# One semaphore step per slot from TensorE in place of one per product, exponent and gather sum, in a vision-tower kernel

## The chip, the cores and the metric

The kernel runs on one core of a Trainium2 chip. The time is the device time of one launch in microseconds, median of the runs shown. TensorE (PE) does the matmuls, ScalarE (ACT) the activations and most evictions, VectorE (DVE) the elementwise work and the searches, GpSimd (POOL) issues the indirect gathers, and SyncE (SP) issues the other DMAs. Each engine runs its own instruction stream; they meet at semaphores only.

## The reference, cut to what matters

There are 64 images of 256 tokens with 64 channels. Each goes through three blocks: a token attention over 4x4 windows (`_L0_tok_ref`), a bidirectional selective scan (`_L0_attn_ref`) and a product-key memory attention (`_L0_ffn_ref`):

```python
h = _L0_tok_ref(x, ...)
h = h + _L0_attn_ref(_layernorm(h), ...)
h = h + _L0_ffn_ref(_layernorm(h), ...)
# in _L0_ffn_ref, for each of 8 heads:
kv_scores, indices = _pk(x, Wq_pk, pk_keys)
k = jnp.einsum('bnhk,bnhkd->bnhd', kv_scores, keys_table[ind])
v = jnp.einsum('bnhk,bnhkd->bnhd', kv_scores, values_table[ind])
out = softmax(causal(q @ k.T)) @ v
```

The third block fills most of the kernel: for each head and token, 16 rows of a table of 4096 are weighted and summed.

## The kernel before

The work is cut into periods of 56 slots, one period per image. In a period every engine works on three images at once: the third block of image b (lead 0), the end of the second block and the search of the third for image b+1, and the first two blocks of image b+2. The tables `FIRST`, `SECOND` and `OWN` say in which slot each engine does which piece of those.

Three and a half of the eight heads are *dense*: instead of gathering rows, TensorE multiplies a table of weights with all rows of the value table. One slot s of this is a chain over two engines:

- `overs` (L907, called o below), the count product: 96x512 bf16 into the bank `zd_ps[s % 2]`. It waits for the keys of the slot (`moving`, loaded by SP) and for the weights of slot s-2, which free the bank.
- `over_limit` (L1158, l below) on ScalarE, in the same bank.
- `exponents` (L913, z below), a second product into that bank, after l. It stands one slot later.
- `weights` (L1164, w below) on ScalarE, the exponential, after z.
- `product_part` (L890, and L896 in the half head at the end; d below), two fp32 products with the table rows `rowtab`, two slots later.

So TensorE's slot s is: z of s-1, o of s, d of s-2, then in 36 of the 56 slots the sums of one gathered part (`gather_sums`, L926, g below), then a stage of the attention over a finished head (`attention`, L940 to L967), then what the tables say. ScalarE's slot s is: w of s-1, in some slots the eviction `keep` (L1171) or `keep_gathered` of a finished head, l of s, a stage of the attention, and the rest.

TensorE tells the others of its progress with four semaphores of the dense and gathered part: `over_mm` steps at each o, `z_ready` at each z, `dense_done` at the second product of each d, and `summed` at the last product of each g. Who waits for them:

- l waits for `over_mm`; w for `z_ready` and for `dense_done` of two slots before (the `weight` buffer); `keep` for `dense_done`; `keep_gathered` for `summed`.
- SP's `load_keys` of slot s (L614 and L617) waits for `z_ready` of slot s-4, whose buffer of four it takes; it stands three slots ahead of its use. `load_tile` (L592) waits for `dense_done`.
- POOL's `gather_image` (L695): before the four gathers of a part it waits for `summed` of the part six before it (`RING` = 6).
- DVE's `spread_weights` waits for `summed` of the previous image.

SP's queue also carries, at slot 13, the load of an image three periods ahead (`load_image`, L578 to L580, three DMAs, 2 MB in all), and behind it in the same queue the keys of slot 16. The stage of slot 47 on TensorE, L814, waits for the end of DVE's scans (L1485).

Of the kernel before, what the change touches and what calls it, by code (L numbers as in the profile page):

```python
# [13 lines left out]
P = 128  # L14
# [21 lines left out]
DENSE = 3  # L36
# [20 lines left out]
WINDOW = (7, 3, 4, 0, 5, 1, 6, 2)  # L57
WSLOTS = 7
CARRIED = 2
# [19 lines left out]
FIRST = """  # L79
0 v.ps a.sq2  # L80
1 a.sq3
2 a.sq0
3 a.sq1
4 p.kv0 a.kv0
5 p.rf v.rf
6 p.kv1 a.kv1 p.kv2 a.kv2
7 p.kv3 a.kv3 p.kv4 a.kv4
8 p.kv5 a.kv5
9 p.kv6 a.kv6 p.kv7 a.kv7
10 p.kv8 a.kv8  # L90
11 p.kv9 a.kv9 p.kv10 a.kv10
12 p.kv11 a.kv11
13 v.var
14 a.rs0
15 v.nw0
16 p.t0 a.t0
17 p.q v.q0
18 v.q1
19 v.q2
20 a.sc  # L100
21 v.pv0
22 v.pv1
23 v.pv2
25 p.t1 a.t1
26 p.pj v.h1
27 a.rs1
28 v.nw1
29 p.t2 a.t2
30 p.xz a.ez
31 v.uz0  # L110
32 a.sg
33 v.uz1
34 p.xd a.xd p.dt a.dt0
35 a.dt1
36 v.dl
37 a.dc0
38 a.dc1 v.B0
39 a.dc2 v.sf0
40 a.dc3 v.sb0
41 a.dc4 v.B1 v.sf1  # L120
42 a.dc5 v.sb1
43 a.dc6 v.B2 v.sf2
44 a.dc7 v.sb2
45 v.B3 v.sf3
46 v.sb3
# [12 lines left out]
59 p.bk
60 v.h2
"""  # L140

SECOND = """
5 v.n0
6 v.n1 a.n
7 p.tb a.tb
8 p.s0 a.s0
9 v.T0 v.T1
10 v.T2 v.T3 p.s1 a.s1
11 v.T4 v.T5 p.s2 a.s2
12 v.T6  # L150
13 v.T7 v.T8 p.s3 a.s3
14 v.T9 v.T10
15 v.T11
16 v.T12 v.T13
19 v.T14
20 v.T15 v.T16
23 v.T17 v.T18
24 v.T19 v.cp v.i a.cp
25 v.pr0 v.L0 v.L1
26 v.L2 v.L3  # L160
27 v.wd v.pr1
28 a.wd
29 v.wx v.sel v.A0 v.G0
30 a.ln p.A0 a.hi0
31 v.A1 v.G1
32 v.re0 v.e0 a.mi0
33 v.G2 p.A1 a.hi1
34 v.e1 v.lo0
35 v.G3 v.re1 a.mi1
36 v.lo1 p.e0 a.e0  # L170
37 v.G4 v.e2 p.e1 a.e1
38 v.wg v.e3 p.e2 a.e2
39 a.wg p.e3 a.e3
40 v.wh
41 a.l2
44 v.R2
46 v.R3
47 v.X5 v.wb0
49 v.R4 v.R5
50 v.A2 v.A3  # L180
51 v.selh
52 v.R6 v.R7
53 v.wb1 v.e4 p.A2 a.hi2
54 v.R8 v.re2 a.mi2
55 v.e5 v.lo2 p.e4 a.e4
"""

OWN = """
0 p.e5 a.e5
1 v.R9 v.e6 p.A3 a.hi3  # L190
2 v.re3 v.R0 v.lo3 a.mi3
3 v.e7 p.e6 a.e6
4 v.R1 v.wb2 v.wb3 p.e7 a.e7
10 v.wb4
"""

# [47 lines left out]
def build(nc, x, wkvT, lnkv, wqT, lnq, projE, w_inT, w_x, w_xT, w_dtT, b_dt, a_log, d_skip,  # L244
# [5 lines left out]
    with ExitStack() as ctx:  # L250
# [1581 lines left out]
```

## Time and profile before

| | |
|---|---|
| median of 3 runs | 17585.84 us |
| range of the runs | 17570.04 to 17600.08 us |
| span of the profiled execution, first to last instruction | 17612.8 us |
| mean granted TensorE clock, share of full speed | 0.823 |
| TensorE busy | 76% |
| VectorE busy | 59% |
| GpSimd busy | 57% |
| ScalarE busy | 42% |
| period (17585.84 us / 64 images) | 275 us |
| slot (275 us / 56) | 4.9 us |

The profile gives the execution's span and no time of its own beside it; the span is 27.0 us (0.15%) over the median of the runs. Engine shares are means over stages with different limits. For a wait, the profile names what ended it and how long the engine had been idle.

### The profile page before, as it was taken

The numbers are of one execution on the slowest core, as the hardware profiler recorded it, in microseconds if no ns is written. First come the engines' busy times: TensorE is split into PE (matmuls) and PEld (weight loads), VectorE is DVE, ScalarE is ACT, GpSimd is POOL, SyncE is SP. The second block draws the span as 40 slices with busy tenths as digits, with TensorE's granted clock in tenths as the row PEclk, the third lists the DMA queues.
The fourth block names the chain that finished last, engine by engine and source line by source line (L and its number), as shares of the span: only waits on it lengthen the run. The fifth ranks groups of instructions, "written<-read, shape, count | busy, mean of one in ns | idle before, by whom it ended". The sixth has DMA issues, their size and how long they took to land.

```text
span 17612.8 us, 261382 instructions
## 1 busy us (share of the span) xinstructions
PE 13397.9 (76%) x71228; PEld 10390.9 (59%) x71228; DVE 10470.6 (59%) x39940; ACT 7416.4 (42%) x17286; POOL 10063.1 (57%) x9220
## 2 busy tenths in 40 slices
PE   4777777777777777777777778777777777777777
PEld 3656556556565555565656656556556665565565
DVE  6656656566566566565665656656656566566562
ACT  2444444444444444444444444444444444344443
POOL 2555555556556556555555556555655555556565
PEclk6888888888888888888888888888888788788888
DMA  2444434444444344343443444444434444344343
GB/s 80 115 114 113 114 108 115 118 110 119 114 112 118 108 115 122 107 116 109 116 117 107 118 111 120 117 113 116 116 108 117 115 112 116 105 116 122 107 116 95
DMA packets 1643030, 1984.06 MB, mean 113 GB/s; under 512 B 527806, under 2 KB 1129022, under 8 KB 1628990
## 3 DMA queue, kind: packets, MB, share of 16 engines
q1 hardware_dynamic: 1346366, 1359.69, 27.2%
q0 software_dynamic: 294912, 604.57, 13.2%
q8 instruction: 665, 10.90, 0.3%
q14 instruction: 1087, 8.90, 0.2%
HBM read 1898.00 MB, written 65.01 MB: 111 GB/s over the span
## 4 chain that ended last, share of the span: by engine, by line
PE 38%; another core or an unknown queue 20%; DVE 15%; issue 13%; ACT 8%; DMA 4%; SPq 1%; DVEq 0%; ACTq 0%
PE bank L890 9%; PE bank L926 6%; DMA moving<-keyspace 4%; PE bank L913 4%; ACT bank L1158 3%; PE bank L907 3%; PE bank L767 2%; PE bank L814 2%; PE bank L875 2%; ACT weight L1164 2%; PE bank L896 1%; PE bank L949 1%; PE bank L851 1%; DVE decay L1484 1%
## 5 line engine op out<-in xcount | busy, mean ns | idle before, releaser
L695 POOL DMA_INDIRECT gath<-in_table_dram,rowsT x9216 | 10062.9, 1092 | 7503.4 <-PE bank L926 3775.8
L890 PE MATMUL bank<-weight,rowtab 128*128 128x256 f32 x12288 | 3919.7, 450 | 0.0
L1164 ACT ACTIVATE weight<-bank 128x512 f32<-128x512 f32 x3584 | 2129.3, 594 | 2782.6 <-PE bank L913 1536.2
L890 PEld LDWEIGHTS bank<-weight,rowtab 128*128 128x128 f32 x12288 | 2814.0, 230 | 825.2 <-issue 196.6
L926 PEld LDWEIGHTS bank<-spread,gath 128*128 128x128 f32 x18432 | 2868.0, 223 | 202.3 <-issue 14.5
L913 PE MATMUL bank<-moving,pick_b 96*128 96x512 bf16 x3584 | 1583.5, 442 | 1730.9 <-ACT bank L1158 1282.0
L926 PE MATMUL bank<-spread,gath 128*128 128x96 f32 x18432 | 2773.9, 301 | 15.6 <-issue 15.3
L1158 ACT ACTIVATE bank<-bank,seventeen 128x512 f32<-128x512 f32 x3584 | 2379.1, 664 | 545.9 <-issue 408.5
L907 PE MATMUL bank<-moving,pick_b 96*128 96x512 bf16 x3584 | 1590.2, 444 | 420.4 <-DMA moving<-keyspace 256.4
L913 PEld LDWEIGHTS bank<-moving,pick_b 96*128 96x128 bf16 x3584 | 400.9, 112 | 2268.3 <-ACT bank L1158 1545.6
L1731 DVE TENSOR_REDUCE negmax<-bank 128x1 f32<-128x128 f32 x512 | 147.8, 289 | 2601.6 <-remote 1389.4
L1474 DVE TENSOR_TENSOR_SCAN decay<-decay,wide 128x1024 f32<-128x1024 f32 x512 | 1162.8, 2282 | 26.3
L1742 DVE SCALAR_TENSOR_TENSOR acc<-bank,rrow,acc 128x64 f32<-128x64 f32 x1024 | 245.3, 278 | 1553.2 <-issue 1080.4
L814 PE MATMUL bank<-decay,ident 128*128 128x256 f32 x2048 | 680.8, 461 | 506.7 <-DVE decay L1485 479.3
L767 PE MATMUL bank<-wkv,pix 128*128 128x130 f32 x4096 | 724.3, 328 | 379.9 <-issue 269.2
L767 PEld LDWEIGHTS bank<-wkv,pix 128*128 128x128 f32 x4096 | 616.1, 228 | 580.0 <-issue 450.9
L1089 ACT ACTIVATE decay<-delta,a_neg 128x255 f32<-128x255 f32 x2048 | 867.3, 503 | 1.7 <-DVE mx L1459 1.7
L814 PEld LDWEIGHTS bank<-decay,ident 128*128 128x128 f32 x2048 | 413.5, 224 | 619.5 <-DVE decay L1485 492.2
L1516 DVE MAX8 best<-sim 128x8 f32<-128x64 f32 x2048 | 281.6, 209 | 807.9 <-ACT sim L1111 785.2
L1054 ACT ACTIVATE wide<-bank 128x390 f32<-128x390 f32 (+1 forms) x768 | 346.3, 461 | 950.6 <-remote 779.3
L1709 DVE TENSOR_TENSOR onehot<-keys_b,idx_b 128x2048 bf16<-128x2048 bf16 x512 | 621.1, 1213 | 155.4 <-remote 136.5
L907 PEld LDWEIGHTS bank<-moving,pick_b 96*128 96x128 bf16 x3584 | 376.6, 105 | 568.6 <-DMA moving<-keyspace 274.7
(266 smaller groups left out, 20279.7 us busy)
## 6 DMA issues: line engine op xcount, KB each, us to landing
rowtab<-in_tableD_dram SPq DMA_DIRECT2D x2048, 256.0 KB
wide<-states SPq DMA_DIRECT2D x512, 512.0 KB
moving<-keyspace SPq DMA_DIRECT2D x3072, 64.0 KB
gath<-in_table_dram,rowsT POOLq DMA_INDIRECT x9216
moving<-keyspace SPq DMA_DIRECT2D x3072, 32.0 KB
pix<-in_x_dram SPq DMA_DIRECT2D x64, 1024.0 KB
pix<-in_x_dram SPq DMA_DIRECT2D x128, 512.0 KB
keyspace<-split SPq DMA_DIRECT2D x192, 256.0 KB, 2.0
```

Source lines behind the costliest of these rows:

```text
L695: pool.indirect_dma_start(out=gath[:, u % RING, j, :], out_offset=None, in_=table, in_offset=bass.IndirectOffsetOnAxis(ap=rowsT[k][:, col: ...
L767: last = mm((scan_ps, misc)[c % 2][:, (n - n0) * KVW:(n - n0 + 1) * KVW], pix[:, n * TOK + t * P:n * TOK + (t + 1) * P], wkv[:], start=Tru ...
L814: mm(scan_ps[:, r * TOK:(r + 1) * TOK], ident[:], decay[r][:, n * TOK:(n + 1) * TOK], start=(n == 0 and r == 0), stop=False, skip_group_ch ...
L890: last = mm(dense_ps[:, 0:TOK], rowtab[:, r, s % 2 * 2 + half, :], weight[s % 2][:, half * TOK:(half + 1) * TOK], start=(s % 16 == 0 and h ...
L907: mm(zd_ps[s % 2][:], pick_b[:, 1, :], moving[r][:], start=True, stop=True, skip_group_check=True).then_inc(over_mm, 1)
L913: mm(zd_ps[s % 2][:], pick_b[:, 0, :], moving[s % KEY_RING][:], start=False, stop=True, skip_group_check=True).then_inc(z_ready, 1)
L926: last = mm(sums_ps[:, col:col + STREAM], gath[:, u % RING, j, :], flat[:, col:col + STREAM], start=True, stop=True)
L1089: last = af(decay[r][:, n * TOK + 1 - r:(n + 1) * TOK - r], delta[:, 1 - r:TOK - r], ACT.Exp, scale=a_neg[:, r * STATE + n:r * STATE + n + 1])
L1158: af(zd_ps[s % 2][:], zd_ps[s % 2][:], ACT.Relu, scale=-BIG, bias=seventeen[:, 0:1]).then_inc(over_ready, 1)
L1164: af(weight[s % 2][:], zd_ps[s % 2][:], ACT.Exp, scale=-1.0).then_inc(weight_ready, 1)
L1474: ins = v.tensor_tensor_scan(d, d, j, 0.0, ALU.mult, ALU.add)
L1709: ins = v.tensor_tensor(hot[:], keys_b[:].unsqueeze(1).to_broadcast([P, 2, KEYS, TOPK]), mine.unsqueeze(2).to_broadcast([P, 2, KEYS, TOPK] ...
```

## The change

All of TensorE's steps for o, z, d and g are replaced by one semaphore, `slot_step`, which steps once per slot, at o. z, d and g step nothing. Whoever waited for one of them now waits for the o that follows it on TensorE. A program that reads TensorE's order (`stands`) gives the count to wait for:

```python
def stands(text):

    where = {}
    for row in text.split("\n"):
        slot, *todo = row.split() or ("",)
        at = [t[0] for t in todo].index("o") if todo else 0
        for i, t in enumerate(todo):
            where[t[:-2]] = int(slot) - int(t[-2:]) * SLOTS + (1 if i <= at else 2)
    return where
```

What stands in a slot before its o is seen at that o, what stands behind it at the o of the next slot. The core of the diff:

```diff
             def overs(b, s):
...
                 mm(zd_ps[s % 2][:], pick_b[:, 1, :], moving[r][:], start=True, stop=True,
-                   skip_group_check=True).then_inc(over_mm, 1)
+                   skip_group_check=True).then_inc(slot_step, 1)
+
+            def empty_slot(b, s):
+
+                if b == IMAGES:
+                    pe.wait_ge(weight_ready, IMAGES * SLOTS - (1 if s == 0 else 0))
+                mm(zd_ps[s % 2][:, 0:1], ident_b[:], ident_b[:, 0:1], start=True, stop=True,
+                   skip_group_check=True).then_inc(slot_step, 1)
 
             def exponents(b, s):
...
-                   skip_group_check=True).then_inc(z_ready, 1)
+                   skip_group_check=True)
...
             def weights(b, s):
 
-                act.wait_ge(z_ready, b * SLOTS + s + 1)
-                wait(act, dense_done, b * SLOTS + s - 1)
+                act.wait_ge(slot_step, seen(b, f"z{s}"))
+                if s >= 2:
+                    wait(act, slot_step, seen(b, f"d{s - 2}"))
...
-                act.wait_ge(dense_done, b * SLOTS + (16 * (h + 1) if h < DENSE else SLOTS))
+                act.wait_ge(slot_step, seen(b, f"d{16 * h + 15 if h < DENSE else SLOTS - 1}"))
...
-                    wait(pool, summed, b * PARTS + (u - RING + 1))
+                    if u >= RING:
+                        wait(pool, slot_step, seen(b, part_name(u - RING)))
+                    elif not isinstance(b, int) or b > 0:
+                        wait(pool, slot_step, seen(b + (-1), part_name(u - RING + PARTS)))
...
-                wait(sp, z_ready, b * SLOTS + s - KEY_RING + 1)
+                if s >= KEY_RING:
+                    wait(sp, slot_step, seen(b, f"z{s - KEY_RING}"))
+                elif not isinstance(b, int) or b > 0:
+                    wait(sp, slot_step, seen(b + (-1), f"z{s - KEY_RING + SLOTS}"))
```

The order of each engine is now written out in full (`PE_ORDER`, `ACT_ORDER`, `DVE_ORDER`, `SP_ORDER`) in place of the three tables, one row per slot; the number behind a name is the lead in images. Two rows of TensorE's:

```python
16 z15+0 o16+0 d14+0 a0.2+0 F.t0+2
17 z16+0 d15+0 o17+0 g1.2+0 a0.3+0 F.q+2
```

In the loops, the instructions of each engine stand as before but for TensorE's slots 1, 17, 33 and 49, where a head ends: there d now stands ahead of o. Slot 17 of TensorE, in the loop (bank0 and bank1 are the two banks of z and o, bank2 that of the products, bank3 the attention's). Before:

```order
L913 MATMUL bank0<-moving0,pick_b 128x512
L907 MATMUL bank1<-moving1,pick_b 128x512
L890 MATMUL bank2<-weight1,rowtab 128x256 x2
L926 MATMUL bank4<-spread2,gath 128x96 x4
L954 MATMUL bank3<-kvg,qT 128x128
L955 MATMUL bank3<-causal_b,ident_b 128x128
L956 MATMUL bank3<-kvg,qT 128x256
L957 MATMUL bank3<-causal_b,ident_b 128x128
L783 MATMUL bank7<-wq,turned 128x72 x2
```

and after (L1032 is z, L1019 o, L1004 d, L1045 g there):

```order
L1032 MATMUL bank0<-moving0,pick_b 128x512
L1004 MATMUL bank2<-weight1,rowtab 128x256 x2
L1019 MATMUL bank1<-moving1,pick_b 128x512
L1045 MATMUL bank4<-spread2,gath 128x96 x4
L1071 MATMUL bank3<-kvg,qT 128x128
L1072 MATMUL bank3<-causal_b,ident_b 128x128
L1073 MATMUL bank3<-kvg,qT 128x256
L1074 MATMUL bank3<-causal_b,ident_b 128x128
L897 MATMUL bank7<-wq,turned 128x72 x2
```

The product of slot 15 and the count product of slot 17 have changed places; nothing else has moved.

In periods without a slot of their own (the two before image 0 and the one after image 63) `empty_slot` keeps the count going, with a product of one column; 168 such products in all. They stand between the pieces of the first two blocks, here in the first period on TensorE (bank6 holds pieces of the second block):

```order
L1026 MATMUL bank0<-ident_b 128x1
L919 MATMUL bank7<-uz,wx_cols 32x256
L915 MATMUL bank6<-uz,w_delta 128x256
L1026 MATMUL bank1<-ident_b 128x1
L1026 MATMUL bank0<-ident_b 128x1
```

The rows of L1026 are new there; the others stood directly behind each other. The loop over pairs of images runs 29 times in place of 30, since two more periods are written out ahead of it.

## Rows read from the trace of the kernel before

**Rows 1.** The page: span, and busy time and instructions of each engine

```profile
span 17612.8 us, 261382 instructions
...
PE 13397.9 (76%) x71228; PEld 10390.9 (59%) x71228; DVE 10470.6 (59%) x39940; ACT 7416.4 (42%) x17286; POOL 10063.1 (57%) x9220
```

**Rows 2.** The page: DMA queues, with packets, MB and share; q0 is the gathers'

```profile
q1 hardware_dynamic: 1346366, 1359.69, 27.2%
q0 software_dynamic: 294912, 604.57, 13.2%
```

**Rows 3.** The waits: engine, line waited for by whom, us, times, longest

```profile
POOL gath L695 <- PE bank L926: 3775.8, 736, 20.0
...
ACT weight L1164 <- PE bank L913: 1536.2, 694, 11.5
...
PE bank L913 <- ACT bank L1158: 1282.0, 611, 9.1
...
PE bank L814 <- DVE decay L1485: 479.3, 68, 31.6
```

**Rows 4.** Groups by line: busy us, mean ns, idle us before, by releaser

```profile
L926 PE MATMUL bank<-spread,gath 128*128 128x96 f32 x18432 | 2773.9, 301 | 15.6 <-issue 15.3
L1158 ACT ACTIVATE bank<-bank,seventeen 128x512 f32<-128x512 f32 x3584 | 2379.1, 664 | 545.9 <-issue 408.5 <-remote 113.0 <-PE bank L907 8.8
L1164 ACT ACTIVATE weight<-bank 128x512 f32<-128x512 f32 x3584 | 2129.3, 594 | 2782.6 <-PE bank L913 1536.2 <-remote 996.8 <-issue 224.0
L907 PE MATMUL bank<-moving,pick_b 96*128 96x512 bf16 x3584 | 1590.2, 444 | 420.4 <-DMA moving<-keyspace 256.4 <-issue 163.9
L913 PE MATMUL bank<-moving,pick_b 96*128 96x512 bf16 x3584 | 1583.5, 442 | 1730.9 <-ACT bank L1158 1282.0 <-issue 408.5 <-ACT weight L1164 31.5
```

**Rows 5.** Timeline of TensorE at full clock: start us, length us, what, idle before

```profile
8004.22 0.39 PE L966 MATMUL bank<-vo,probT 128*128 128x64 f32 x2
8004.44 0.39 PE L967 MATMUL bank<-vo,probT 128*128 128x64 f32 x2
8004.67 0.38 PE L913 MATMUL bank<-moving,pick_b 96*128 96x512 bf16 x1
8004.89 0.38 PE L907 MATMUL bank<-moving,pick_b 96*128 96x512 bf16 x1
```

**Rows 6.** Timeline of TensorE, slots 46 and 47 of one image

```profile
5947.30 0.38 PE L913 MATMUL bank<-moving,pick_b 96*128 96x512 bf16 x1
5947.52 0.38 PE L907 MATMUL bank<-moving,pick_b 96*128 96x512 bf16 x1
5947.74 1.03 PE L890 MATMUL bank<-weight,rowtab 128*128 128x256 f32 x4
5948.93 0.39 PE L913 MATMUL bank<-moving,pick_b 96*128 96x512 bf16 x1 [0.16 <-ACT bank L1158]
```

**Rows 7.** Timeline of ScalarE, the same stretch

```profile
5947.72 0.60 ACT L1164 ACTIVATE weight<-bank 128x512 f32<-128x512 f32 x1 [0.96 <-issue]
5948.21 0.66 ACT L1158 ACTIVATE bank<-bank,seventeen 128x512 f32<-128x512 f32 x1
```

**Rows 8.** Timeline of TensorE behind slot 47, the wait for the scans

```profile
5962.17 2.08 PE L814 MATMUL bank<-decay,ident 128*128 128x256 f32 x4 [7.64 <-DVE decay L1485]
```

**Rows 9.** Timeline of TensorE, slots 16 to 18 of that image

```profile
5803.75 0.39 PE L913 MATMUL bank<-moving,pick_b 96*128 96x512 bf16 x1 [0.79 <-issue]
5810.92 0.61 PE L907 MATMUL bank<-moving,pick_b 96*128 96x512 bf16 x1 [6.78 <-issue]
...
5814.64 0.63 PE L913 MATMUL bank<-moving,pick_b 96*128 96x512 bf16 x1
5815.07 0.63 PE L907 MATMUL bank<-moving,pick_b 96*128 96x512 bf16 x1
5815.49 1.91 PE L890 MATMUL bank<-weight,rowtab 128*128 128x256 f32 x4
5817.20 1.30 PE L926 MATMUL bank<-spread,gath 128*128 128x96 f32 x8
...
5820.15 0.38 PE L913 MATMUL bank<-moving,pick_b 96*128 96x512 bf16 x1
...
5822.54 0.38 PE L907 MATMUL bank<-moving,pick_b 96*128 96x512 bf16 x1
```

**Rows 10.** Timeline of ScalarE, slot 17 (w, keep, l)

```profile
5815.31 0.60 ACT L1164 ACTIVATE weight<-bank 128x512 f32<-128x512 f32 x1
5817.50 0.38 ACT L1171 ACTIVATE kvd<-bank 128x256 f32<-128x256 f32 x1 [1.60 <-PE bank L890]
5817.78 0.66 ACT L1158 ACTIVATE bank<-bank,seventeen 128x512 f32<-128x512 f32 x1
```

**Rows 11.** Timeline of SP's queue: image load, keys of slots 16 and 19

```profile
5795.57 0.55 SPq L578 DMA_DIRECT2D pix<-in_x_dram  x1
...
5797.56 0.62 SPq L614 DMA_DIRECT2D moving<-keyspace  x1
...
5804.32 0.58 SPq L614 DMA_DIRECT2D moving<-keyspace  x1
```

**Rows 12.** Timeline of POOL: the gathers of the part behind slot 15

```profile
5807.62 0.95 POOL L695 DMA_INDIRECT gath<-in_table_dram,rowsT  x1 [0.30 <-issue]
5808.87 0.94 POOL L695 DMA_INDIRECT gath<-in_table_dram,rowsT  x1 [0.30 <-issue]
```

**Rows 13.** Stretches: busy us of each engine, then clock, DMA share, GB/s

```profile
5807.00:5811.00 4.00, 0.08 (x1) 0.09 (x2) 2.30 (x18) 0.00 (x0) 3.09 (x4) 0.57 1.06 250
...
0.00:293.00 293.00, 90.02 (x400) 66.32 (x400) 206.14 (x710) 66.55 (x155) 26.86 (x25) 0.64 0.25 68
```

**Rows 14.** The chain that ended last, pieces behind slot 17

```profile
5820.77 2.30 DVE decay L1394
...
5862.42 3.33 another core or an unknown queue
```

More of the change, by code:

```diff
@@ L76 @@
 PAIRS = _pos
[L79 to L113, printed above, removed]
@@ L154 @@
[L154 to L184, printed above, removed]
@@ L211 @@
-PLAN = [schedule(FIRST, 1, 2), schedule(SECOND, 2, 1), schedule(OWN, 2, 0)]
-def pieces(engine, s, first, second, own):
-    on = {2: first, 1: second, 0: own}
-    todo = [p for part in (PLAN[1], PLAN[2], PLAN[0]) for p in sorted(part[s], key=lambda p: p[0])]
-    return [(lead, stage, name) for lead, stage, e, name in todo if e == engine and on[lead]]
+PE_ORDER = """
+0 z55-1 o0+0 d54-1 a6.0-1 S.e5+0 F.y+1
+1 z0+0 d55-1 o1+0 S.A3+0 F.g+1
+2 z1+0 o2+0 d0+0 g0.0+0 a6.2-1
+3 z2+0 o3+0 d1+0 g0.1+0 a6.3-1 S.e6+0 F.bk+1
@@ new lines @@
+2 S.re3+0 S.R0+0 S.lo3+0 F.g+1
+3 a6.3-1 S.e7+0
+4 S.R1+0 S.wb2+0 S.wb3+0 F.h2+1
+5 a6.5-1 S.n0+1 F.rf+2
+6 a6.6-1 S.n1+1
+7
+8
+9 S.T0+1 S.T1+1
+10 a7.3-1 S.T2+1 S.T3+1 S.wb4+0
+11 S.T4+1 S.T5+1
+12 a7.5-1 S.T6+1
+13 a7.6-1 S.T7+1 S.T8+1 F.var+2
+14 S.T9+1 S.T10+1
+15 S.T11+1 F.nw0+2
+16 S.T12+1 S.T13+1
+17 a0.3+0 F.q0+2
+18 F.q1+2
+19 a0.5+0 S.T14+1 F.q2+2
+20 a0.6+0 S.T15+1 S.T16+1
+21 F.pv0+2
+22 F.pv1+2
+23 S.T17+1 S.T18+1 F.pv2+2
+24 a1.3+0 S.T19+1 S.cp+1 S.i+1
+25 S.pr0+1 S.L0+1 S.L1+1
+26 a1.5+0 S.L2+1 S.L3+1 F.h1+2
@@ new lines @@
+51 S.selh+1 F.C3+2
+52 a5.3+0 S.R6+1 S.R7+1
+53 S.wb1+1 S.e4+1
+54 a5.5+0 S.R8+1 S.re2+1
+55 a5.6+0 S.e5+1 S.lo2+1
+"""
+SP_ORDER = """
+0 t2+0 m3+0
+1 st2+0 m4+0
+2 t3+0 m5+0
+3 m6+0
+4 t4+0 m7+0
+5 st3+0 m8+0
+6 t5+0 m9+0
+7 m10+0
+8 t6+0 m11+0
+9 m12+0
+10 t7+0 m13+0
+11 m14+0
+12 t8+0 m15+0
+13 x+3 m16+0
+14 t9+0 m17+0
+15 out-1 m18+0
+16 t10+0 m19+0
+17 m20+0
+18 t11+0 m21+0
+19 m22+0
+20 t12+0 m23+0
+21 m24+0
+22 t13+0 m25+0
+23 m26+0
+24 t14+0 m27+0
+25 m28+0
+26 t15+0 m29+0
+27 m30+0
+28 t16+0 m31+0
@@ new lines, with planned @@
+29 m32+0
+30 t17+0 m33+0
+31 m34+0
+32 t18+0 m35+0
+33 m36+0
+34 t19+0 m37+0
+35 bc+2 m38+0
+36 t20+0 m39+0
+37 m40+0
+38 t21+0 m41+0
+39 m42+0
+40 st0+1 st1+1 t22+0 m43+0
+41 m44+0
+42 lq0+2 t23+0 m45+0
+43 m46+0
+44 lq1+2 t24+0 m47+0
+45 t25+0 m48+0
+46 lq2+2 t26+0 m49+0
+47 t27+0 m50+0
+48 lq3+2 t28+0 m51+0
+49 t29+0 m52+0
+50 t30+0 m53+0
+51 t31+0 m54+0
+52 t0+1 m55+0
+53 m0+1
+54 t1+1 m1+1
+55 m2+1
+"""
+def planned(text):
+    rows = [row.split() for row in text.split("\n") if row]
+    return [(t[:-2], int(t[-2:])) for _, *todo in rows for t in todo]
@@ L680, in _ @@
+            for b in range(-LEAD, 3):
+                period(b, b % 2)
+            with sp.Fori(0, (IMAGES - 6) // 2) as i:
+                period(i * 2 + 3, 1)
+                period(i * 2 + 4, 0)
+            for b in range(IMAGES - 3, IMAGES + 1):
+                period(b, b % 2)
             sp.wait_ge(stored, 16 * IMAGES)
@@ L1006, in _ @@
+            prepare()
+            for b in range(-LEAD, 3):
+                period(b, b % 2)
+            with pe.Fori(0, (IMAGES - 6) // 2) as i:
+                period(i * 2 + 3, 1)
+                period(i * 2 + 4, 0)
+            for b in range(IMAGES - 3, IMAGES + 1):
+                period(b, b % 2)
         @block.scalar
```

476 lines of the change are left out of this document (261 added, 215 removed).

## The prediction

> **What bounds the kernel now.** I read the page first. TensorE is busy for 76% of the span and VectorE for 59% [rows 1], so no engine fills it, and what counts is who waits for whom. The waits come next. TensorE's exponent product z waits 611 times for ScalarE's l, 1282 us in all; ScalarE's w waits 694 times for z, 1536 us; POOL waits 736 times for a gather sum, 3776 us; the product behind slot 47 waits 68 times for VectorE's scans, 479 us [rows 3]. Last come timelines of one image, to see which of these stand one behind the other. The reader is to see three kinds of stretch. In some, the chain z, w, l, z over TensorE and ScalarE is tight [rows 6, 7]. In others TensorE stands still for something far away: 6.8 us in slot 16 for keys that lie behind the image load [rows 9], 7.6 us behind slot 47 for the scans [rows 8]. In the rest ScalarE comes late to work that has long been ready, or TensorE has other work.
>
> **Steps taken away.** Per image z, d and g stepped 56, 56 and 36 times: 148 x 64 = 9472 steps fewer. Does a step cost TensorE time? At full clock L966 has two passes and no step, and the next product starts 0.22 us after it; L967 has the same shape, two passes and a step, and the next starts 0.23 us after it. z and o, 512 columns each, follow at 0.22 us with a step on both [rows 5]. So a step costs between 0 and 0.01 us, the last digit of the rows. As an upper bound that is 9472 x 0.01 = 95 us of gain if all lay on the path. I take 0, since the distances with and without a step agree to that digit, and 512 columns at 2.4 GHz are 0.21 us by themselves.
>
> The Trainium skill ("TensorE: Matmul & The Clock Gate", section "The cost: per-tile semaphore tail") says otherwise, for small tiles packed into the array: increments serialize at about 26.3 ns each. By that, an estimate would be 9472 x 26.3 ns = 249 us of gain. The rows above disagree for products that follow one another.
>
> **w waits for o.** w of slot s waited for z and now waits for the o behind it. o starts 0.22 us after z at full clock, 0.43 us at half clock (5815.07 - 5814.64) [rows 5, 9]. At a mean clock of 0.823 some 35% of the time is at half clock, so a w that waits is later by 0.65 x 0.22 + 0.35 x 0.43 = 0.29 us. l stands behind w and moves with it. Only where w waited for z, and TensorE's next z then waited for l, does TensorE lose this. The upper bound is all 611 waits of z: 611 x 0.29 = 177 us. The lower bound comes from what I find tight: in slots 46 and 47 of the image shown z starts at 5947.30, w at 5947.72, l at 5948.21, and the next z at 5948.93, idle until l [rows 6, 7]. This would be 0.22 us per image, and slot 18 has about the same pattern (o at 5822.54, one slot of 1.6 us), so 64 x 0.44 = 28 us. But the first stands ahead of the wait of 7.64 us for the scans, which no product of slot 46 feeds [rows 8]; it is taken up there. The second stands behind the start of VectorE's own chain, which runs from 5820.77 to 5862.42 [rows 14]; it is taken up too. What is left are irregular cases in slots 22 to 37. I take 15 us, near the lower end, between 0 and 177.
>
> **d ahead of o.** In four slots per image o comes later by d, 4 passes: 5817.20 - 5815.49 = 1.71 us at half clock, half of that at full. In slot 17 that gives o at 5816.78 and w at 5817.2. keep waited for d until 5817.50; behind w it starts at about 5817.8, and l ends at 5818.8 in place of 5818.44. The next z started only at 5820.15 because of the work between [rows 9, 10], so TensorE loses nothing there. In slots 1 and 33 it may. Bounds are 0 and 256 x 0.5 = 128 us (0.5 us is w standing ahead of keep, since the two starts of w and l in rows 7 are 0.49 us apart); I take 10 us, since slot 17 shows more than 1 us to spare.
>
> **POOL's gathers come later.** A part of gathers is now released at the o of the next slot. POOL is not pressed: the sums waited for gathers hardly at all, 15.6 us in the whole run [rows 4], and a release that is a slot later (4.9 us) is small against the nine slots (six parts at 1.5 slots) between the issue of a part and its use. So no cost, as long as the margin holds. There is one gain. In slot 16 TensorE waits for keys issued at 5797.56, right behind the 2 MB of the image load issued from 5795.57; they have landed at 5810.92 [rows 9, 11]. Meanwhile POOL issues the part released by the sum of slot 15, at 5807.62 and 5808.87 [rows 12], and the DMA engines are full: share 1.06, 250 GB/s [rows 13]. This part will now wait for o of slot 16, that is until after the stall. A gather carries 604.57 MB / 9216 = 66 kB [rows 2]; 9216 is 36 parts x 4 gathers x 64 images, so two of them out of the way give 131 kB / 250 GB/s = 0.52 us, times 62 images 32 us. A gain could reach twice that if the whole part counts (four gathers); it could be 0 if the gathers don't slow the image load. I take 16 us, the middle of 0 and 32.
>
> **SP's loads come later.** The keys of a slot are issued at o in place of z, 0.2 to 0.4 us later, against three slots of lead. The keys of slot 19 were issued at 5804.32, during the stall, and will be issued after 5810.92, for use at 5822.54 or a little later [rows 9, 11]: 11.6 us, against 13.4 us that the keys of slot 16 took behind the image load. The same length again would cost 1.8 us x 62 = 112 us; but by then the load has ended, so I take 0 and keep 112 us as an end.
>
> **The ends of the program.** 168 products of one column, most of them in the first 293 us, where TensorE is busy for only 90 us [rows 13]; at the 0.11 us of a pass (two in 0.22 us [rows 5]) 18 us at most, hidden beside VectorE's 206 us. I take 0. One loop turn less for two written-out periods is the same instructions.
>
> **The sum.** 0 + 15 + 10 - 16 + 0 + 0 = +9 us. On the profiled span, 17612.8 + 9 = 17621.8 us; the median of the runs is 27.0 us under the span, which gives 17595 us. A measurement of this kernel can tell about 0.2%, 35 us, from no change.
>
> **The rivals.**
>
> *The longer chain is passed on.* l is later in every tight slot, and ScalarE's other work behind it moves too; a late vo or probability moves VectorE, whose queue is in order. For it: 694 waits of w for z and 611 of z for l, of similar number. Against it: ScalarE sat idle 2783 us before w [rows 4], and the tight slots I find stand ahead of longer waits. At 0.15 to 0.29 us for 611 waits it gives +90 to +177 us; it decides from about 200 passed waits on (35 / 0.177). With the middle of it, 0.18 us, and no other term: 17586 + 110 = 17696 us. Chance 0.22.
>
> *The gathers or keys come too late.* The release waits through the stalls, and a later part or key makes TensorE wait. For it: the keys of slot 19 have 11.6 us. Against it: 15.6 us of waits for gathers, and nine slots. By the end above: 17586 + 112 = 17698 us. Chance 0.08.
>
> *The DMA stall gets shorter by the whole part, and fewer steps help a little.* 64 us from four gathers, less the 15 and 10 us: 17586 - 39 = 17547 us. For it: the DMA share of 1.06. Against it: the last two of the four are issued at the end of the stall or behind it. Chance 0.14.
>
> *The steps did cost TensorE time.* As a mechanism of this kernel, 0.01 us for each of 9472 steps: 17586 - 95 = 17491 us. The rows of L966 and L967 leave room for it, those of z and o hardly. The page of the Trainium skill named above states this rule. Chance 0.06.
>
> *The change does less than it says*, because w is mostly released by ScalarE's own queue: that is the forecast itself, and gives no change.
>
> **How the numbers follow.** No change that can be told, 17551 to 17621 us: 0.50. Slower: 0.22 + 0.08 = 0.30. Faster: 0.14 + 0.06 = 0.20. The forecast is the likeliest case, 17595 us. The range reaches down to 17535 us, so that the shorter stall is in and the cost of steps is out, and up to 17690 us, which holds about half of the two slower cases. Left out is some 0.06 below and 0.14 above.
>
> **What would show it.** Right: w is now released by o (L907's successor), starts some 0.2 us later where it waits, and z's waits for l grow by less than 60 us; the stall of slot 16 is shorter by half a microsecond; POOL's waits for sums turn into waits for o; the wait behind slot 47 shrinks by about 0.2 us each. Wrong: z's waits for l grow by 100 us or more and the other waits don't shrink (the first rival); TensorE shows waits for gathers or for keys in slot 19 (the second); distances between products without steps are shorter than with them (the last).

## The result and the profile after

The changed kernel takes 17437.31 us, median of 4 runs (17417.39 to 17451.7), beside 17577.94 us for the kernel before (17549.95 to 17600.08). The ratio is 0.9919, 95% interval 0.9898 to 0.994: some 141 us faster, where 17595 us and no difference were forecast. It lies below the range.

The page of the changed kernel, span and busy time, the chain that ended last, and the gathers (columns as in [rows 4]):

```profile
span 17449.9 us, 261002 instructions
...
PE 13138.8 (75%) x71396; PEld 10190.3 (58%) x71396; DVE 10498.7 (60%) x39940; ACT 7404.0 (42%) x17286; POOL 10111.3 (58%) x9220
...
PE 31%; DVE 25%; issue 17%; another core or an unknown queue 17%; ACT 8%; DVEq 0%; DMA 0%; SPq 0%; ACTq 0%
...
L809 POOL DMA_INDIRECT gath<-in_table_dram,rowsT x9216 | 10111.1, 1097 | 7294.1 <-PE bank L1019 3529.0
```

The groups by line of the changed kernel: w, z, l, o, then the products that wait for ScalarE's `wide`, for VectorE's `acc` and for VectorE's `nrm`:

```profile
L1279 ACT ACTIVATE weight<-bank 128x512 f32<-128x512 f32 x3584 | 2136.2, 596 | 3494.4 <-PE bank L1019 1928.7 <-remote 1034.5 <-issue 517.5
L1032 PE MATMUL bank<-moving,pick_b 96*128 96x512 bf16 x3584 | 1575.4, 440 | 1728.5 <-ACT bank L1272 1294.2 <-issue 284.2 <-ACT weight L1279 132.0
L1272 ACT ACTIVATE bank<-bank,seventeen 128x512 f32<-128x512 f32 x3584 | 2376.7, 663 | 7.9 <-issue 1.6
L1019 PE MATMUL bank<-moving,pick_b 96*128 96x512 bf16 x3584 | 1557.8, 435 | 23.7 <-issue 13.0 <-DMA moving<-keyspace 10.1
...
L881 PE MATMUL bank<-wkv,pix 128*128 128x130 f32 x4096 | 602.6, 290 | 63.0 <-ACT wide L1168 51.7 <-issue 7.4 <-ACT pix L1163 3.1
...
L1057 PE MATMUL bank<-xT,wq_ffn 64*64 64x256 f32 x1024 | 392.2, 469 | 531.4 <-DVE acc L1854 404.9 <-issue 116.8 <-remote 9.0
...
L866 PE MATMUL bank<-ident,nrm 128*64 128x128 f32 x384 | 94.2, 337 | 698.1 <-DVE nrm L1460 628.2 <-DVE nrm L1541 45.5 <-issue 22.0
```

The last three in the kernel before:

```profile
L767 PE MATMUL bank<-wkv,pix 128*128 128x130 f32 x4096 | 724.3, 328 | 379.9 <-issue 269.2 <-ACT wide L1054 104.4 <-ACT pix L1049 5.4
...
L940 PE MATMUL bank<-xT,wq_ffn 64*64 64x256 f32 x1024 | 375.1, 451 | 241.3 <-issue 151.1 <-DVE acc L1742 83.9 <-remote 5.8
...
L752 PE MATMUL bank<-ident,nrm 128*64 128x128 f32 x384 | 96.2, 342 | 93.8 <-DVE nrm L1429 45.1 <-DVE nrm L1348 35.6 <-issue 7.6
```

Beside [rows 4]: w waits longer, 3494.4 us against 2782.6, and for o, as the diff says; so does GpSimd, whose gathers waited 3775.8 us for sums [rows 3] and now wait 3529.0 us for o (L1019). z's waits for l hardly grow, 1294.2 us against 1282.0 [rows 3]. TensorE's idle time before o, 420.4 us, is nearly gone (23.7 us), and so is that before the products that wait for `wide` (379.9 us, now 63.0 us). But TensorE now stands 698.1 us before the transposes of `nrm` (93.8 us before) and 531.4 us before L1057, which waits for `acc` (241.3 us before); VectorE makes both. TensorE's idle time, span less busy time, even grows, from 17612.8 - 13397.9 = 4214.9 us [rows 1] to 17449.9 - 13138.8 = 4311.1 us. The gain stands wholly in its busy time, 259 us less; the granted clock rises from 0.823 to 0.836 of full speed. So waits have moved, and TensorE spends more of its work at the higher clock.

Per slot (from the start of one z to the next, mean over images 3 to 60) an image takes 271.84 us before and 269.05 us after. Slots 6, 9 and 10 give 9.6 us per image; slot 13 takes back 5.7 us, slot 54 2.7 us, and slots 28 and 29 another 2.7 us. (Slot s runs here from the z of slot s to the z of slot s+1, so the o of slot 16 lies in slot 15.) Two stretches stand out: slots 6 to 9 take 26.8 us before and 18.4 us after, slots 12 to 15 20.1 us before and 27.3 us after. Neither is in the prediction's sum.

**What the prediction had not seen.** Releaser "remote" in [rows 4] is a wait whose end the profile can't put down to a local event. Here is one such place in the kernel before, in slot 9 of one image, the timeline (start us, length us, engine, line, idle before). First GpSimd:

```profile
5771.94 0.94 POOL L695 DMA_INDIRECT gath<-in_table_dram,rowsT  x1 [7.36 <-PE bank L926]
5773.19 0.94 POOL L695 DMA_INDIRECT gath<-in_table_dram,rowsT  x1 [0.30 <-issue]
...
5780.69 0.94 POOL L695 DMA_INDIRECT gath<-in_table_dram,rowsT  x1 [0.30 <-issue]
```

TensorE in the same stretch, up to its own stop:

```profile
5776.73 0.38 PE L913 MATMUL bank<-moving,pick_b 96*128 96x512 bf16 x1
...
5779.33 0.23 PE L957 MATMUL bank<-causal_b,ident_b 128*128 128x128 bf16 x1
...
5783.92 0.80 PE L767 MATMUL bank<-wkv,pix 128*128 128x130 f32 x2 [3.31 <-ACT wide L1054]
```

And those who waited for it:

```profile
5783.37 0.88 ACT L1054 ACTIVATE wide<-bank 128x390 f32<-128x390 f32 x2 [5.42 <-remote]
5783.47 0.58 SPq L614 DMA_DIRECT2D moving<-keyspace  x1
5783.65 0.29 DVE L1731 TENSOR_REDUCE negmax<-bank 128x1 f32<-128x128 f32 x1 [7.87 <-remote]
```

Eight gathers run back to back from 5771.94 to 5781.63 us. z at 5776.73 is over by 5777.1, L957 by 5779.6. Yet SyncE, which waits for that z, VectorE, which waits for L957, and ScalarE all wake within 0.3 us of each other, at 5783.4 to 5783.7. TensorE's steps were made, and seen up to 6.5 us late, all at once, 1.7 us after the last gather was issued. The trace also keeps arrivals of steps, the times at which a semaphore's new value is recorded. Set beside the end of the instruction that makes them, TensorE's come 14 to 15 ns behind it when they are on time, and 26% of those recorded come over 2 us late in the kernel before. Of ScalarE's and VectorE's it is 0.9% each (for ScalarE that is no sign of lateness: it has 0.7% where nothing else is late). Stretches in which a step of TensorE is over 0.5 us late add up to 6316 us in 1168 places before and 5859 us in 1329 after. (Part of the arrivals isn't on record, so such sums are good to some per cent.) This became the theory to test: GpSimd's series of gathers (a series: gathers issued with some 0.3 us between one and the next) decide when TensorE's steps are seen, and the change moved the series.

### The profile page after: what moved, and what is told of

It is laid out like the page before. It is cut to its first block, busy times and chain, and to the rows that moved or that the text cites. A ratio compares the mean times of both kernels' runs of the same rounds, so it can differ in the third digit from the quotient of the medians.

```text
span 17449.9 us, 261002 instructions
## 1 busy us (share of the span) xinstructions
PE 13138.8 (75%) x71396; PEld 10190.3 (58%) x71396; DVE 10498.7 (60%) x39940; ACT 7404.0 (42%) x17286; POOL 10111.3 (58%) x9220
## 4 chain that ended last, share of the span: by engine, by line
PE 31%; DVE 25%; issue 17%; another core or an unknown queue 17%; ACT 8%; DVEq 0%; DMA 0%; SPq 0%; ACTq 0%
PE bank L1004 7%; PE bank L1045 5%; ACT bank L1272 3%; PE bank L1032 3%; PE bank L1019 3%; ACT weight L1279 2%; PE bank L989 2%; PE bank L928 2%; DVE best_i L1636 2%; PE bank L881 2%; DVE best_i L1630 2%; DVE decay L1596 1%; DVE apart L1722 1%; DVE left L1632 1%
## 5 line engine op out<-in xcount | busy, mean ns | idle before, releaser
L809 POOL DMA_INDIRECT gath<-in_table_dram,rowsT x9216 | 10111.1, 1097 | 7294.1 <-PE bank L1019 3529.0
L1004 PE MATMUL bank<-weight,rowtab 128*128 128x256 f32 x12288 | 3806.2, 439 | 0.7 <-issue 0.7
L1279 ACT ACTIVATE weight<-bank 128x512 f32<-128x512 f32 x3584 | 2136.2, 596 | 3494.4 <-PE bank L1019 1928.7
L1004 PEld LDWEIGHTS bank<-weight,rowtab 128*128 128x128 f32 x12288 | 2741.2, 224 | 771.3 <-issue 167.8
L1045 PEld LDWEIGHTS bank<-spread,gath 128*128 128x128 f32 x18432 | 2790.2, 218 | 204.0 <-issue 30.8
L1032 PE MATMUL bank<-moving,pick_b 96*128 96x512 bf16 x3584 | 1575.4, 440 | 1728.5 <-ACT bank L1272 1294.2
L1045 PE MATMUL bank<-spread,gath 128*128 128x96 f32 x18432 | 2702.2, 296 | 9.8 <-issue 9.2
L1032 PEld LDWEIGHTS bank<-moving,pick_b 96*128 96x128 bf16 x3584 | 399.5, 111 | 2313.6 <-ACT bank L1272 1618.8
L1019 PE MATMUL bank<-moving,pick_b 96*128 96x512 bf16 x3584 | 1557.8, 435 | 23.7 <-issue 13.0
L1057 PE MATMUL bank<-xT,wq_ffn 64*64 64x256 f32 x1024 | 392.2, 469 | 531.4 <-DVE acc L1854 404.9
L1010 PEld LDWEIGHTS bank<-weight,rowtab 128*128 128x128 f32 x4096 | 616.5, 216 | 122.2 <-issue 63.2
L881 PE MATMUL bank<-wkv,pix 128*128 128x130 f32 x4096 | 602.6, 290 | 63.0 <-ACT wide L1168 51.7
L881 PEld LDWEIGHTS bank<-wkv,pix 128*128 128x128 f32 x4096 | 514.7, 196 | 229.1 <-issue 147.7
```

Source lines behind the costliest of these rows:

```text
L809: pool.indirect_dma_start(out=gath[:, u % RING, j, :], out_offset=None, in_=table, in_offset=bass.IndirectOffsetOnAxis(ap=rowsT[k][:, col: ...
L881: last = mm((scan_ps, misc)[c % 2][:, (n - n0) * KVW:(n - n0 + 1) * KVW], pix[:, n * TOK + t * P:n * TOK + (t + 1) * P], wkv[:], start=Tru ...
L1004: mm(dense_ps[:, 0:TOK], rowtab[:, r, s % 2 * 2 + half, :], weight[s % 2][:, half * TOK:(half + 1) * TOK], start=(s % 16 == 0 and half == ...
L1019: mm(zd_ps[s % 2][:], pick_b[:, 1, :], moving[r][:], start=True, stop=True, skip_group_check=True).then_inc(slot_step, 1)
L1032: mm(zd_ps[s % 2][:], pick_b[:, 0, :], moving[s % KEY_RING][:], start=False, stop=True, skip_group_check=True)
L1045: mm(sums_ps[:, col:col + STREAM], gath[:, u % RING, j, :], flat[:, col:col + STREAM], start=True, stop=True)
```

## The experiments

The kernel before was timed beside each. Its time had two levels, and the second was not expected at all:

| occasion | kernel before, us | TensorE's arrivals over 2 us late | kernels beside it |
|---|---|---|---|
| late steps | 17577.94; 17333.42; 17359.34 | 23 to 28%; 1.3% with half the gathers | after; c1, e8, e9; e7b, e1c, e3c, c2 |
| no late steps | 14326.28; 14319.19; 14315.77 | 0.1% | e1 to e4; e7, e10, e1b, e3b; e11 to e13 |

One chip showed both levels, 17333.42 us and later 14315.77 us, so the level is no property of a chip. All ratios are to the kernel before on the same occasion.

**The parts of the change, without late steps.** e1: GpSimd alone waits for the count product.

```diff
-                    wait(pool, summed, b * PARTS + (u - RING + 1))
+                    at = 2 + 3 * (u - RING) // 2 if u >= RING else 2 + 3 * (u - RING + PARTS) // 2 - SLOTS
+                    wait(pool, over_mm, b * SLOTS + at + 2)
```

> The kernel before, with one edit: GpSimd waits before each part of gathers for the count product of the slot behind the sum, in place of the sum itself. All steps stay. Gather theory (the gain of 141 us comes from when the gathers run: TensorE's steps are seen 1 to 8 us late while eight gathers follow one another, and the release decides where that falls): 70 to 140 us faster, ratio 0.992 to 0.996, the wait of 6.8 us for the keys of slot 16 is gone, and GpSimd's idle time before a gather ends at the count product. Step theory (fewer steps of TensorE are what helps): ratio 0.999 to 1.001. My prediction's own term for this edit was 16 us.

Measured 1.0018 (1.0009 to 1.0027), and again 1.0019 (1.0007 to 1.003). The waits for keys are still there, against the expectation:

```profile
L908 PE MATMUL bank<-moving,pick_b 96*128 96x512 bf16 x3584 | 1452.9, 405 | 658.5 <-DMA moving<-keyspace 654.2 <-ACT weight L1165 4.3
```

e2: the changed kernel, its last gather sum stepping `summed` again, and GpSimd waiting for that. (Of the 148 steps per image 112 stay away; the 92 of the text below is a slip.)

```diff
-                    mm(sums_ps[:, col:col + STREAM], gath[:, u % RING, j, :],
-                       flat[:, col:col + STREAM], start=True, stop=True)
+                    last = mm(sums_ps[:, col:col + STREAM], gath[:, u % RING, j, :],
+                              flat[:, col:col + STREAM], start=True, stop=True)
+                last.then_inc(summed, 1)
```

> The changed kernel, with one edit: the last gather sum of a part steps a semaphore again, and GpSimd alone waits for it. 92 of the 148 steps per image stay away, d stays ahead of the count product in four slots, w and the key loads wait for the count product. Gather theory: the gain is lost, ratio to the kernel before 0.996 to 1.0, and TensorE waits for the keys of slot 16 again. Step theory: the gain stays, ratio 0.992 to 0.994.

Measured 0.9987 (0.9976 to 0.9998). e3: the changed kernel with steps of their own on z, d and the sums, for which nobody waits; that of z (d and the sums likewise):

```diff
-                   skip_group_check=True)
+                   skip_group_check=True).then_inc(z_told, 1)
```

> The changed kernel, with one edit: z, d and the gather sums step three semaphores of their own again, for which nobody waits. The number of steps is that of the kernel before, everything else that of the changed one. Gather theory: ratio to the kernel before 0.991 to 0.993, as the changed kernel. Step theory: 0.997 to 1.0. If each step took the time that the Trainium skill gives for increments of packed tiles, it would be 249 us slower than the changed kernel, ratio 1.006.

Measured 1.0003 (0.9987 to 1.0018), and again 1.0018 (1.0008 to 1.0029). e4: d ahead of o in slots 1, 17, 33 and 49 alone.

```diff
-                    if main:
+                    if main and s % 16 != 1:
                         overs(b, s)
...
+                    if main and s % 16 == 1:
+                        overs(b, s)
```

> The kernel before, with one edit: in slots 1, 17, 33 and 49 TensorE does the products d ahead of the count product, as in the changed kernel. Gather and step theory: nothing, ratio 0.999 to 1.001; my prediction gave it 10 us of loss, between 0 and 128. Order theory (d first lets the finished head be evicted sooner, and the attention behind it starts sooner): ratio 0.993 to 0.997.

Measured 1.0011 (1.0001 to 1.0021). Both theories of e1 to e3 are missed here: no edit moves more than 0.2%. The reason is in the table above. On this occasion no step is late, and the waits of e1 have not one row with the releaser "remote". Long series of gathers are there all the same, and longer ones than with late steps: e1 has 60 series of 100 gathers and more, without a late step in them. So a long series alone delays nothing; something that differs between occasions has to be there as well.

**The change itself again, and the series of gathers made longer and thinner.** These met late steps. c1 is the changed kernel.

> The changed kernel itself, unaltered, beside the kernel before. In the runs of the first four experiments the kernel before took 14326 us in place of 17578 us, and none of TensorE's steps was seen late (over half a microsecond) once the loops ran, where the first traces had over 1100 stretches of lateness, 6316 us in all. If the gain of 0.8% hangs on these late steps (theory of late steps), it is absent here: ratio 0.999 to 1.001, as for the changed kernel with its steps put back (1.0003). If it hangs on something that is there on both occasions (the wait for keys in slot 16, fewer steps), ratio 0.991 to 0.994.

Measured 0.997 (0.9954 to 0.9986). The premise of its text, an occasion without late steps, didn't hold. e8: 16 gathers in a row.

```diff
-                    wait(pool, summed, b * PARTS + (u - RING + 1))
+                    if u % 4 == 0:
+                        wait(pool, summed, b * PARTS + (u + 3 - RING + 1))
```

> The kernel before, with one edit: GpSimd waits only before every fourth part, for the sum of the part three behind, so that 16 gathers follow one another where it was 8. Gather theory (TensorE's steps are seen late for as long as a series of gathers lasts): slower by over 2% where steps are late at all, with freezes of up to 19 us; where they aren't, the rival says the gathers only crowd the DMA engines: ratio 0.998 to 1.01. No theory expects it faster by more than 0.2%.

Measured 1.1219 (1.1189 to 1.1249). Its longest "remote" waits are those of a longer series:

```profile
ACT weight L1165 <- remote: 1424.3, 319, 17.3
ACT split L1152 <- remote: 1303.9, 111, 15.1
DVE negmax L1732 <- remote: 1122.6, 97, 20.6
```

In the same stretch of the run 16 gathers run from 5766.04 to 5785.77 us in e8, and steps are late from 5774.10 to 5789.19: 15.1 us at one stroke. Over the run, 401 series of 16 or more have 18.0 us of lateness each (60 of them are 48 long). e9: half the gathers; the sums read the two that are there twice, so the kernel leaves out half of the gathered rows.

```diff
-                    for j in range(PART):
+                    for j in range(2):
```

> The kernel before, with two of the four gathers of each part left out; the sums read the two that are there twice. Gather theory: if steps are late on the chip of this run, the time falls by over 5% (17578 towards 14300 us) and the late stretches shrink to under 2 us each. Where steps are not late, the DMA engines have 15% less to do: 0 to 1% faster, by shorter waits for keys (654 us in all before the count product).

Measured 0.8179 (0.8153 to 0.8206), 14178.76 us: below the time of the whole kernel where no steps are late, on an occasion where the kernel before takes 17333.42 us. "Remote" waits are nearly gone (largest rows: 204.7 us, 59.3 us):

```profile
ACT split L1151 <- remote: 204.7, 61, 4.0
DVE onehot L1709 <- remote: 59.3, 58, 1.6
```

Late stretches add up to 657 us. That e9 has a tenth of the lateness and not half of it speaks for the series and not for each gather: its gathers come in twos (1588 series, 0.36 us of lateness each). The rival, less load on the DMA engines, was given up to 1%. But length is not the whole of it. e9 also has 321 series of four, and they carry 0.25 us of lateness each, where series of four in e1c below carry 2 us. Half the gathers is also half of what they move, and whether that counts beside the length was not tried apart.

**Spread gathers.** e7 was to release the eight gathers of two parts as 3, 3 and 2.

```diff
                     for j in range(PART):
+                        late = j == 3 if u % 2 == 0 else j > 1
+                        if j == 0 or late:
+                            wait(pool, over_mm, b * SLOTS + at + 2 + ((2 if u % 2 == 0 else 1) if late else 0))
+                            pool.sem_inc(held, 1)
```

It and its like on the changed kernel (e10) first met no late steps:

> The kernel before, with GpSimd's eight gathers of a pair of parts released 3, 3 and 2 by the count products of three slots in a row, in place of 4 and 4 by two sums, so that fewer follow one another at once. Gather theory: on a chip where TensorE's steps are seen late (the kernel before near 17300 us) 3 to 15% faster, late stretches in all under 3000 us against 5600 to 6300; on one where they are not (near 14326 us) ratio 0.998 to 1.003. Rival (the load on the DMA engines, not the length of the series): no change on either, 0.998 to 1.002.

> The changed kernel, with the gathers spread 3, 3 and 2 as in the experiment on the kernel before. Gather theory: the same gain as there, so that the two kernels differ by less than 0.3%. If the changed kernel had an advantage of its own (fewer steps), it would stay 0.3 to 0.8% ahead of the spread kernel before.

Measured 1.0006 (0.9997 to 1.0015) and 1.0014 (1.0004 to 1.0025). The repeats of e1 and e3 given above ran beside them.

> The kernel of the first experiment again (GpSimd alone waits for the count product, all steps kept). On a chip where steps are seen late, gather theory: 0.992 to 0.998, as the changed kernel; step theory: 0.999 to 1.001. On one where they aren't: 1.002, as measured.

> The changed kernel with its steps put back, again. On a chip where steps are seen late, gather theory: 0.992 to 0.998, as the changed kernel; step theory (more steps, more to deliver behind a freeze): 0.999 or above. On one where they aren't: 1.000, as measured.

The edit does not make that pattern, whatever the occasion. The fourth gather of an even part waits for the count `at + 4`. The odd part behind it has an `at` that is one higher, and waits for its own `at + 2` and `at + 3`, that is for nothing later than the fourth gather has waited for. So the release is 3 and then 5. Five gathers take some 6.2 us, and the next 3 are released one slot later, 4.9 us: they follow on, and the series has eight. The repeat with late steps:

> The spread gathers on the kernel before, again, since the last runs met no late steps. On a chip where the kernel before takes about 17300 us, gather theory (a freeze needs a long series): 0.85 to 0.97; rival (the number of gathers in flight or the load counts, not the series): 0.99 to 1.01. Without late steps: 1.0006 as measured.

Measured 1.0282 (1.0257 to 1.0306): slower, against every expectation. The trace shows the pattern of the edit: 586 series of exactly eight gathers, which begin at the fourth gather of an even part, 195 of five and 185 of three, and none of four, where the kernel before has 484 of eight and 382 of four. A series of eight carries 7.05 us of lateness there, one of five 2.4 us, one of three 0.44 us. So the run is no test of spread gathers, which remains to be done. It is one of longer series, and it fits the theory that they cost.

**The parts of the change, with late steps, side by side.**

> GpSimd alone waits for the count product, again. Where steps are seen late, gather theory: 0.992 to 0.998, as the changed kernel in the same run; step theory: 0.999 to 1.001. Where they aren't: 1.002, as measured twice.

> The changed kernel with its steps put back, again. Where steps are seen late, gather theory: the ratio of the changed kernel in the same run within 0.002; step theory: 0.003 or more above it. Where they aren't: 1.000 to 1.002, as measured twice.

> The changed kernel, unaltered, again. Where steps are seen late: 0.991 to 0.998. Where they aren't: 0.999 to 1.002, since its twin with the steps put back has 1.0003 and 1.0018 there; a ratio below 0.998 there would speak for a cost of the steps themselves.

| kernel | ratio, 95% interval | series of exactly 4 gathers | late stretches, us |
|---|---|---|---|
| e1c, release of gathers alone | 0.9775 (0.9752 to 0.9799) | 613 | 5714 |
| c2, the whole change | 0.9973 (0.9957 to 0.9988) | 611 | 5537 |
| e3c, the whole change, steps put back | 0.9985 (0.997 to 1.0) | 639 | 6492 |

The later release of the gathers alone gains 393 us, more than the whole change on any occasion. Putting 148 steps per image back adds 0.0012 or 21 us to the ratio, with overlapping intervals that allow up to 0.0043 or 75 us. And something else in the change takes 2% back. Sums of lateness don't tell what, since e1c has more of it than c2: it matters where in the image it falls. The groups by line of e1c and of c2 show where the time stands. e1c:

```profile
L1165 ACT ACTIVATE weight<-bank 128x512 f32<-128x512 f32 x3584 | 2129.6, 594 | 2647.9 <-PE bank L914 1505.8 <-remote 667.7 <-issue 450.3
...
L908 PE MATMUL bank<-moving,pick_b 96*128 96x512 bf16 x3584 | 1562.7, 436 | 143.8 <-DMA moving<-keyspace 77.4 <-issue 65.0 <-ACT weight L1165 0.8
L941 PE MATMUL bank<-xT,wq_ffn 64*64 64x256 f32 x1024 | 389.0, 466 | 328.1 <-DVE acc L1743 214.0 <-issue 98.5 <-remote 13.4
L753 PE MATMUL bank<-ident,nrm 128*64 128x128 f32 x384 | 90.3, 324 | 216.3 <-DVE nrm L1349 145.2 <-DVE nrm L1430 39.5 <-issue 30.6
```

c2:

```profile
L1279 ACT ACTIVATE weight<-bank 128x512 f32<-128x512 f32 x3584 | 2134.1, 595 | 3462.5 <-PE bank L1019 1971.5 <-remote 879.3 <-issue 599.0
...
L1019 PE MATMUL bank<-moving,pick_b 96*128 96x512 bf16 x3584 | 1552.6, 433 | 21.7 <-issue 16.0 <-DMA moving<-keyspace 4.9
L1057 PE MATMUL bank<-xT,wq_ffn 64*64 64x256 f32 x1024 | 396.3, 474 | 494.4 <-DVE acc L1854 402.7 <-issue 89.8
L866 PE MATMUL bank<-ident,nrm 128*64 128x128 f32 x384 | 91.9, 330 | 659.5 <-DVE nrm L1460 589.3 <-DVE nrm L1541 46.3 <-issue 21.6
```

ScalarE's w waits 815 us longer in c2, but ScalarE has idle time. TensorE stands 443 us longer before `nrm` in c2 than in e1c (659.5 - 216.3), 166 us longer before the product that waits for `acc`, and 122 us less before keys. The table has the time of the two stretches of the image, from the start of z to the start of z:

| kernel | slots 6 to 9, us | slots 12 to 15, us | whole image, us |
|---|---|---|---|
| before (first occasion) | 26.8 | 20.1 | 271.8 |
| e1c | 17.8 | 20.3 | 261.4 |
| c2 | 18.3 | 26.4 | 267.0 |
| e3c | 18.3 | 26.5 | 267.6 |
| after, c1 | 18.4, 18.6 | 27.3, 26.1 | 269.1, 266.2 |

In slots 6 to 9 every kernel of the table with the later release is 8 to 9 us faster than the kernel before, e1c with nothing but that edit too. There the kernel before waits for `wide` in slots 6 and 9, some 6 us per image, and the place shown above is one of these waits. In slots 12 to 15 all traces of the changed kernel take 6 to 7 us more than e1c and the kernel before. There TensorE waits for VectorE: in c2 4.9 us per image for `acc` in slot 13 and 8.0 us for `nrm` in slot 15, in e1c 1.5 and 0.9 us. These 6.1 us are more than the 5.6 us that lie between e1c and c2. e3c has it too, so the number of steps is not its cause. Why VectorE is late there isn't shown. The kernel before was kept as a trace of the first occasion only, so its row stands beside the others with that reserve.

**What takes it back.** w waiting for o (e11), d ahead of o (e12) and the keys released at o (e13) were each put on top of e1. e12 is the edit of e4; the edits of e11 and e13:

```diff
-                act.wait_ge(z_ready, b * SLOTS + s + 1)
+                if isinstance(b, int) and b == IMAGES - 1 and s == SLOTS - 1:
+                    act.wait_ge(z_ready, b * SLOTS + s + 1)
+                else:
+                    act.wait_ge(over_mm, b * SLOTS + s + 2)
...
-                wait(sp, z_ready, b * SLOTS + s - KEY_RING + 1)
+                wait(sp, over_mm, b * SLOTS + s - KEY_RING + 2)
```

> The kernel of the first experiment (later release of the gathers), and ScalarE's w waits for the next count product in place of z. Theory that w's wait takes the 2% back: 0.990 to 0.998 where steps are seen late, against 0.978 without the edit. Rivals (d first, or the keys): 0.976 to 0.981. Where steps aren't late: 1.000 to 1.004.

> The kernel of the first experiment, and d stands ahead of the count product in slots 1, 17, 33 and 49. Theory that this takes the 2% back (it moves the release of gathers and of ScalarE's l by up to 1.7 us in four slots): 0.990 to 0.998 where steps are seen late. Rivals: 0.976 to 0.981. Where steps aren't late: 1.001 to 1.004, since it alone gave 1.0011 there.

> The kernel of the first experiment, and SyncE's key loads are released by the next count product in place of z. Theory that keys released later take the 2% back: 0.990 to 0.998 where steps are seen late, with TensorE waiting for keys again. Rivals: 0.976 to 0.981. Where steps aren't late: 1.001 to 1.003.

They met no late steps: 1.0033 (1.002 to 1.0046), 1.0022 (1.0012 to 1.0031) and 1.0026 (1.0017 to 1.0035), against 1.0018 and 1.0019 of e1 on other occasions. At most w's wait shows, by 0.0014 or 20 us, with intervals that overlap. Which of the three, or which of them together, costs 2% where steps are late stays open.

## Why the prediction was wrong

**The premise of every term.** The prediction took each wait to end when the work waited for ends, so it priced releases by distances of 0.22 to 0.43 us. On the occasions of its trace this failed for TensorE's steps, of which a quarter is seen over 2 us late. [rows 4] showed it: 996.8 us of w's 2782.6 us ended by "remote". I read the part that ended by z and passed over that word. On the occasions without late steps no part comes to more than 0.2%. The steps of the prediction that failed are this premise and, in the sum, the next term.

**POOL's gathers come later, -16 us, between 0 and -64.** This is the term that failed. "POOL is not pressed" was right and beside the point. Not what GpSimd waits for but when it runs sets the time: the release alone is worth -391 us by e1c (17359.34 x 0.0225) with late steps, and +26 us without (e1). (On the occasion of the result itself the release was not timed alone; but the trace there has the same gain in slots 6 to 9, 8.4 us per image.) Its mechanism, two gathers out of the way of the image load, was not the one: without late steps TensorE's waits for keys are 637.2 us in e4, with the release at the sum, and 654.2 us in e1, with the release at o. With late steps the idle time before o went from 420.4 us to 23.7 us after and 143.8 us in e1c, but the stall was not shortened: from the z of slot 12 to the o of slot 16 an image takes 16.3 us before and 16.5 us after. TensorE only reaches that o later, since it has waited for `acc` in slot 13 by then, and behind it it waits for `nrm`. Both waits for VectorE are in no term.

**Steps taken away, 0.** Right as far as the runs can tell. The steps put back give 0.9985 against 0.9973, and without late steps 1.0003 and 1.0018. The 249 us that were estimated from the Trainium skill ("TensorE: Matmul & The Clock Gate", section "The cost: per-tile semaphore tail") would be a ratio 0.014 higher with the steps back. The runs, with 0.0043 at most, rule it out for these products, which follow one another and aren't packed.

**w waits for o, +15 us.** z's waits for l grew by 12 us, as forecast; without late steps e11 gives some 20 us. Under late steps it wasn't measured alone.

**d ahead of o, +10 us.** e4 gives 0.0011 x 14326 = 16 us (1 to 30) without late steps.

**SP's loads, 0.** e13 gives 0.0007 more than e1, 10 us, within the intervals.

**The sum, +9 us**, a ratio of 1.0005, matches what the changed kernel with its steps put back shows without late steps (1.0003, 1.0018). The changed kernel itself was not timed there. That match is in part luck: the term for the gathers was -16 us, and e1 gives +26 us there. With late steps it is 0.9919, 0.997 and 0.9973: always a gain, and a small rest of two larger effects of opposite sign, -2.25% and +2%. Why the rest is 141 us on one occasion and 50 and 58 us on the others isn't known; the kernel before itself took 17578 us on the first and 17333 and 17359 us on the others.

**The rivals.** The longer chain (17696 us) did not come about as priced, since z's waits did not grow. (Its price has a slip: the middle of 0.15 and 0.29 us is 0.22 us and not 0.18 us, which gives 134 us in place of 110 us.) Something like it did happen by another way, though: VectorE is later in slots 12 to 15, and TensorE waits for it. Of the shorter stall only the sign of the whole was right, and that by luck: the stall ends no sooner. A rival in which the timing of the gathers changes what others see was missing, and 0.14 + 0.06 for faster was too little for it.

**The version that beats both where steps are late** is e1: one wait changed in the kernel before. With late steps it was timed on one occasion, 16966.36 us beside 17359.34 us and 17300.93 us; without them it costs 0.2%.

## What to carry to other kernels

If the profile puts waits down to "remote" though one core alone runs, look at the timeline whether several engines wake in the same instant, and what GpSimd was doing until then. In such a kernel, try software gathers in short series, count in the trace whether they came out short, and judge the release of gathers by what it does to everyone's waits, not by whether GpSimd has time. And look at the time of the unchanged kernel on each occasion before a ratio of under 1% is explained: here it had two levels 21 to 23% apart, and the parts of the change meant different things on each.

## What the runs showed of the hardware

- On some occasions TensorE's semaphore steps are seen late, all at once, while GpSimd issues indirect gathers back to back. In a series of eight the latest step is 5.3 us late in the kernel before and 5.7 us in e7b, with 16 gathers 14.7 us in e8 (medians). Lateness per series: 0.36 us for two (e9), 0.44 us for three and 2.4 us for five (e7b), 2 us for four in e1c but 0.25 us in e9, 6 to 7 us for eight. Without the condition, series of over 100 gathers have none (e1). ScalarE's and VectorE's steps are hardly touched (of VectorE's at most 2.3% over 2 us late, e8).
- The page "Perfetto Trace Analysis" of the Trainium skill says, in its section on per-engine timelines, that a semaphore update takes time to reach all engines and that this time isn't in the profile's instruction. The runs agree: an arrival stands 14 to 15 ns behind the end of TensorE's instruction when it is on time, and up to 6.5 us in the place shown. Nothing on the page ties it to gathers.
- The gathers themselves don't start or issue more slowly: in both conditions the first packet of a gather starts 1.7 us after its issue (median, kernel before and e1), and GpSimd takes 1092 and 1101 ns for one.
- The effect comes and goes: of six occasions three had it, and one chip had both. What switches it on is not known. All runs here were recorded by the profiler, and under late steps fewer arrivals of steps are on record (68% of ScalarE's, against 99%). The missing arrivals go with the occasion more than with the lateness: e9, with next to none late, has 84% of ScalarE's on record, and e8, with the most lateness, 75%. Whether the recording has a part in it was not tried.
